# Sending the last seventeen weight blocks of a mixture-of-experts tail from the ScalarE queue

## What is computed

```python
hn2 = _layernorm(x, ln2_g, ln2_b).reshape(-1, h)
logits = hn2 @ gate_w + gate_b
idx = jnp.argmax(logits, axis=-1)
mid = jax.nn.relu(jnp.einsum('th,ehf->etf', hn2, w1) + b1[:, None, :])
y = jnp.einsum('etf,efh->eth', mid, w2) + b2[:, None, :]
moe = y[idx, jnp.arange(hn2.shape[0])]
return x + moe.reshape(b, s, h)
```

## Time and profile before

| | |
|---|---|
| median of 3 timed runs | 705.04 us (702.55 to 707.58) |
| profiled execution, its own time | 702.71 us |
| span in the profile | 701.0 us |
| mean granted TensorE clock | 0.927 |

### The profile page before, as it was taken

The page is one execution under the profiler, slowest core; times in us unless marked ns, Lnnn a source line. Parts: engine busy times, 40 slices in busy tenths (PEclk is TensorE's granted clock), DMA queues, the critical chain, the costliest instruction groups (busy, mean ns, idle before and its releaser), DMA issues.

```text
span 701.0 us, 16358 instructions
## 1 busy us (share of the span) xinstructions
PE 570.1 (81%) x5771; PEld 339.1 (48%) x5771; DVE 480.9 (69%) x1356; ACT 425.4 (61%) x650; POOL 416.7 (59%) x443
## 2 busy tenths in 40 slices
PE   2648888888888878888897898878997899888992
PEld 1324333344445444455454554545553555557992
DVE  3546757868678868587867768687777787635452
ACT  1675376676785666757677596756675654534661
POOL 2469573648486953775757585769544235525664
PEclk9969779899999988799999999899998999999996
DMA  6420000000000100000012301001002022186650
GB/s 146 135 69 2 8 1 9 2 24 1 9 2 25 40 2 6 5 16 10 17 41 62 85 9 36 1 20 60 25 29 62 12 69 91 39 257 183 187 149 6
DMA packets 30143, 34.30 MB, mean 49 GB/s; under 512 B 6970, under 2 KB 21984, under 8 KB 30064
## 3 DMA queue, kind: packets, MB, share of 16 engines
q1 hardware_dynamic: 26096, 25.53, 12.9%
q0 software_dynamic: 2816, 6.43, 2.6%
q10 hardware_dynamic: 1152, 1.30, 0.6%
HBM read 22.37 MB, written 11.27 MB: 48 GB/s over the span
## 4 chain that ended last, share of the span: by engine, by line
PE 40%; DVE 23%; POOL 16%; issue 10%; ACT 7%; SPq 2%; DMA 1%; POOLq 0%; ACTq 0%; DVEq 0%
DVE mx L1230 10%; PE out L877 6%; POOL rs L1411 5%; PE ring_s L863 3%; POOL stack L1414 3%; PE out L762 3%; PE ring_p L943 3%; PE ring_p L701 3%; PE ring_s L843 3%; POOL p L1430 2%; ACT p L1004 2%; PE ring_p L814 2%; ACT p L973 2%; PE ring_s L749 2%; PE ring_p L931 1%
## 5 line engine op out<-in xcount | busy, mean ns | idle before, releaser
L1230 DVE TENSOR_REDUCE mx<-ring_s 128x4 f32<-128x1024 f32 x128 | 152.8, 1218 | 26.9 <-PE ring_s L843 26.1
L1004 ACT ACTIVATE p<-ring_s 128x1024 f32<-128x1024 f32 x128 | 126.3, 1027 | 38.8 <-PE ring_s L863 38.3
L973 ACT ACTIVATE p<-ring_s 128x1024 f32<-128x1024 f32 x96 | 97.1, 1022 | 38.5 <-PE ring_s L749 38.1
L1411 POOL TENSOR_TENSOR rs<-ms,small 128x40 f32<-128x40 f32 x14 | 94.8, 6772 | 27.6 <-DVE ms L1093 27.3
L1414 POOL TENSOR_SCALAR stack<-stack 128x256 f16<-128x256 f16 (+1 forms) x96 | 65.0, 700 | 75.7 <-DVE stack L1222 42.8
L1430 POOL TENSOR_SCALAR_AFFINE_SELECT p<-p 128x512 f32<-128x512 f32 (+1 forms) x96 | 75.8, 798 | 56.4 <-ACT p L977 56.3
L977 ACT ACTIVATE p<-p 128x1024 f32<-128x1024 f32 x96 | 100.2, 1057 | 0.7
L701 PE MATMUL ring_p<-blank 128*128 128x256 f16 x362 | 80.6, 286 | 5.1 <-ACT t_midT L1037 1.9
L877 PE MATMUL out<-p,v 128*32 128x256 f32 x1024 | 69.8, 400 | 1.3 <-DVE rb L1288 1.2
L843 PE MATMUL ring_s<-kc,qs 32*128 32x256 f16 x512 | 51.2, 281 | 20.2 <-DVE mx L1230 13.0
L863 PE MATMUL ring_s<-qs,kc 32*128 32x256 f16 x512 | 49.4, 290 | 10.1 <-DMA qs<-mT 4.5
(11 more groups left out here) (162 smaller groups left out, 1111.5 us busy)
## 6 DMA issues: line engine op xcount, KB each, us to landing
w_up<-in_L_ffn_w SPq DMA_DIRECT2D x40, 256.0 KB, 2.8
t_row<-routed_rows SPq DMA_DIRECT2D x40, 132.0 KB, 2.4
routed_rows<-padrow SPq DMA_DIRECT2D x8, 396.0 KB, 3.2
xs<-in_L_attn_x SPq DMA_DIRECT2D x16, 128.0 KB, 2.2
routed_rows<-padrow SPq DMA_DIRECT2D x8, 132.0 KB, 1.9
qs<-mT SPq DMA_DIRECT2D x64, 2.0 KB
out<-t_y,t_idx POOLq DMA_INDIRECT x40, 2.4
b_down<-in_L_ffn_b SPq DMA_DIRECT2D x1, 512.0 KB, 4.8
```

The costliest lines, as they stand in the source:

```text
L973: nc.scalar.activation(p1[:, u], bank(f"b_sc{u}", n)[:], ACT.Tanh, scale=float(ISQ / CAP)).then_inc(b_s.sem, 1)
L1004: nc.scalar.activation(p2[:, u], bank(f"e_sc{u}", n)[:], ACT.Exp, scale=float(ISQ)).then_inc(e_s.sem, 1)
L1230: nc.vector.tensor_reduce(mx2[:, t, 2 * pair:2 * pair + 2, 2 * k:2 * k + 2], bank(f"d_mx{j}", n)[:].rearrange("p (z g s) -> p z g s", z=2, ...
L1411: nc.gpsimd.tensor_tensor(rs1[:], ms1[:], half, ALU.pow).then_inc(a_p.sem, 1)
```

## The change

The up weights of tiles 23 to 39 are no longer sent by SyncE (`g_w`) but by ScalarE, in a new step `g_wa`. It waits for the plan and for the up product of tile s-8, as `g_w` does, reads the expert's number into a ScalarE register, sends the transfer, and keeps the register; `g_mid` of the same tile then uses it and does not read the number again.

```diff
-ONLY = dict(a_root=tuple(range(ROOTS)), a_pow=tuple(range(ROOTS, B)), p_bT=(0,), p_bTc=(0,), p_plan=tuple(last for last, *_ in PLANS), q_sp=(PLANS[-2][0],))
+ONLY = dict(g_w=tuple(range(PLANS[-1][1])), g_wa=tuple(range(PLANS[-1][1], SLOTS)), a_root=tuple(range(ROOTS)), a_pow=tuple(range(ROOTS, B)), p_bT=(0,), p_bTc=(0,), p_plan=tuple(last for last, *_ in PLANS), q_sp=(PLANS[-2][0],))
...
+            expert = {}
+
+            def g_wa(s):
+                act.wait_ge(r_v.sem, r_v.upto(LAST, "row"))
+                wait(act, up_t, s - 8, "x")
+                expert[s] = act.value_load(slots[0:1, 0, s:s + 1], min_val=0, max_val=E - 1)
+                act.dma_start(w_up[:, s % 8, :], w1_d[bass.ds(expert[s] * P, P), :]).then_inc(w_in[s % 8], 16)
+
             def g_mid(s):
                 if s == 0:
                     act.wait_ge(bias_s.sem, bias_s.upto(0, "x"))
-                e = act.value_load(slots[0:1, 0, s:s + 1], min_val=0, max_val=E - 1)
+                if s in expert:
+                    e = expert[s]
+                else:
+                    e = act.value_load(slots[0:1, 0, s:s + 1], min_val=0, max_val=E - 1)
...
+    "g_wa": (2630, 2631, 2638, 2651, 2657, 2695, 2698, 2708, 2710, 2729, 2741, 2758, 2769, 2782, 2800, 2811, 2830),
```

More of the change, by code:

```diff
@@ new lines @@
+    "a_sum": (7, 24, 82, 131, 277, 421, 543, 708, 879, 1025, 1183, 1314, 1458, 1667, 1825, 1933),
+    "a_xT": (9, 14, 22, 102, 130, 286, 408, 569, 726, 937, 1051, 1179, 1309, 1503, 1658, 1807),
+    "a_qkv": (12, 19, 57, 124, 232, 382, 534, 687, 840, 1000, 1132, 1287, 1437, 1628, 1789, 1900),
+    "a_root": (15, 31),
+    "a_split": (16, 39, 98, 191, 297, 437, 595, 747, 909, 1112, 1215, 1393, 1536, 1697, 1860, 1992),
+    "a_qT": (23, 51, 118, 220, 319, 462, 614, 771, 943, 1122, 1246, 1416, 1594, 1734, 1876, 2017),
@@ new lines @@
+    "g_w": (1487, 1506, 1562, 1633, 1634, 1642, 1816, 1821, 2106, 2148, 2183, 2205, 2251, 2253, 2276, 2291, 2297,
+        2540, 2541, 2546, 2555, 2633, 2640),
+    "g_hTc": (1514, 1535, 1674, 1703, 1765, 1868, 1943, 1993, 2128, 2221, 2332, 2336, 2405, 2440, 2464, 2473, 2474,
+        2564, 2567, 2598, 2608, 2637, 2652, 2666, 2676, 2696, 2703, 2709, 2716, 2720, 2730, 2736, 2754, 2780, 2785,
+        2794, 2802, 2822, 2840, 2844),
+    "g_hT": (1519, 1533, 1673, 1688, 1770, 1852, 1923, 1979, 2120, 2231, 2338, 2342, 2401, 2442, 2458, 2467, 2471,
+        2568, 2582, 2601, 2614, 2628, 2648, 2663, 2678, 2688, 2707, 2714, 2723, 2735, 2740, 2748, 2760, 2772, 2776,
+        2784, 2796, 2805, 2817, 2826),
@@ new lines @@
+    "g_up": (1542, 1560, 1707, 1843, 1907, 1962, 1991, 2099, 2152, 2304, 2352, 2364, 2411, 2449, 2480, 2507, 2534,
+        2589, 2592, 2620, 2624, 2642, 2667, 2682, 2689, 2706, 2718, 2725, 2737, 2745, 2753, 2761, 2768, 2777, 2788,
+        2804, 2813, 2829, 2835, 2838),
+    "g_mid": (1546, 1547, 1709, 1857, 1908, 1957, 2001, 2097, 2165, 2298, 2345, 2379, 2423, 2447, 2478, 2518, 2533,
+        2573, 2581, 2617, 2626, 2650, 2670, 2683, 2700, 2702, 2715, 2724, 2734, 2749, 2750, 2765, 2781, 2793, 2798,
+        2812, 2842, 2845, 2851, 2853),
@@ new lines @@
+    "g_down": (1645, 1654, 1799, 1864, 1989, 2092, 2110, 2115, 2182, 2312, 2388, 2433, 2450, 2497, 2525, 2552, 2558,
+        2593, 2616, 2625, 2636, 2658, 2685, 2693, 2712, 2721, 2739, 2752, 2755, 2766, 2767, 2775, 2783, 2792, 2808,
+        2818, 2831, 2836, 2848, 2855),
+    "g_z": (1653, 1668, 1822, 1886, 2002, 2085, 2118, 2124, 2227, 2318, 2400, 2448, 2463, 2503, 2544, 2557, 2561,
+        2599, 2611, 2644, 2649, 2659, 2681, 2684, 2691, 2704, 2719, 2743, 2746, 2757, 2763, 2779, 2790, 2791, 2814,
+        2823, 2827, 2847, 2849, 2858),
@@ new lines @@
+    "g_rs": (1694, 1761, 1850, 1949, 2019, 2078, 2130, 2170, 2224, 2392, 2395, 2454, 2456, 2510, 2520, 2559, 2577,
+        2585, 2635, 2646, 2660, 2668, 2680, 2692, 2694, 2728, 2733, 2738, 2770, 2771, 2787, 2799, 2810, 2815, 2819,
+        2832, 2837, 2843, 2852, 2860),
+    "g_y": (1721, 1846, 1911, 1969, 2051, 2091, 2210, 2242, 2271, 2421, 2434, 2498, 2506, 2528, 2554, 2578, 2609,
+        2634, 2645, 2647, 2653, 2661, 2686, 2699, 2713, 2717, 2732, 2751, 2762, 2764, 2778, 2786, 2806, 2820, 2824,
+        2828, 2846, 2850, 2857, 2859),
@@ L308 @@
+    "g_out": (1797, 1906, 1946, 2027, 2084, 2129, 2261, 2373, 2413, 2476, 2488, 2509, 2512, 2516, 2574, 2580, 2606,
+        2664, 2665, 2675, 2687, 2690, 2701, 2711, 2722, 2731, 2747, 2756, 2774, 2797, 2803, 2809, 2816, 2821, 2834,
+        2839, 2841, 2854, 2856, 2861),
+    "q_sp": (2613,),
+    "g_wa": (2630, 2631, 2638, 2651, 2657, 2695, 2698, 2708, 2710, 2729, 2741, 2758, 2769, 2782, 2800, 2811, 2830),
 }
@@ L1042, in _ @@
             parts = dict(a_xTc=a_xTc, c_sum=c_sum, c_oTc=c_oTc, d_xTc=d_xTc, d_mTc=d_mTc, f_sum=f_sum, f_oTc=f_oTc,
-                         f_hTc=f_hTc, p_bTc=p_bTc, g_hTc=g_hTc, g_mid=g_mid)
+                         f_hTc=f_hTc, p_bTc=p_bTc, g_hTc=g_hTc, g_mid=g_mid, g_wa=g_wa)
             numbered(parts, "b_tanh", 6, b_tanh)
```

161 lines of the change are left out of this document (64 added, 97 removed), and 171 rows, old and new, of the table ORDER.

## The result

| | before | changed |
|---|---|---|
| median, four runs of each on one chip | 703.79 us (701.01 to 707.58) | 715.34 us (713.87 to 717.77) |
| profiled execution: own time, span | 702.71, 701.0 us | 713.87, 712.1 us |

The ratio is 1.0164, with a 95% interval from 1.0106 to 1.0222: slower by 11.6 us, and 3.3 us outside the range of the forecast. On another chip the same two kernels turned out level; that comes with the experiments.

A forecast was written before the change was run, and what follows sets the result against it. TensorE was taken as next to full in the tail, no single cost as the steady part's bound. Terms -0.3 + 1.4 + 0 + 0 - 2 = -0.9 from 702.7 gave 701.8; with 2.3 for timed runs, 704 us, range 696 to 712.

The forecast's parts named there:

- What bounds the kernel: Tail: TensorE next to full, 2.48 us a tile, no waits for weights; steady part: no one cost is the bound.
- SyncE's relief: Tail: SyncE loses 17 weight sends, worth nothing for weights; tile 23's row-block wait shrinks by 0 to 1.1 us, taken as -0.3.
- ScalarE's sends, +1.4 us: Tail: 17 sends on ScalarE at mean net 0.33 us each, a quarter of it reaching TensorE: +1.4 us.
- The rival that made them the tail's bound: Tail: each of the 17 sends delays g_hTc or g_mid by 0.65 us, +11 instead of +1.4: 714 us, chance 0.12.
- the fillers' rival: Ahead of batch 7's maxima: some 36 more fillers cost their 8 us, without the clock's gain: 714 us; 0.06 with unlucky order.
- The order at the last plan: VectorE: up 20's wait for g_z of tile 18 goes, the plan comes later; 1.8 us gained against 1.8 lost, 0.
- Pads: SyncE's q_sp comes 3.5 us later behind three more sends; spare before the last scatter shrinks from 4.1 to 0.6 us: 0.
- Fillers and clock from 40 to 100 us: Start: more and earlier fillers raise TensorE's low clock, 7.8 us less busy time, a quarter of it taken: -2 us.
- The rest of the order: 0: All engines: new order not priceable by rows; work ahead of each batch's maxima differs by at most 22 steps: 0, several us each way.
- the case that would put the result down to the steady part: Sign of being wrong: the last plan moves by more than 5 us, so the steady part's order, not any term, made the result.

The follow-up runs named there:

- queue_only: Kernel before, old order, with only the 17 weight sends of tiles 23 to 39 moved to ScalarE: 1.0000 of the kernel before, then 1.0016 on chip 9.
- plan_first: Changed kernel with VectorE's last plan put ahead of g_y of tile 16 and g_z of tile 18: 0.9940 of the kernel before, again (plan_first_2) 1.0161.
- the clean pair on chip 5: Changed kernel with VectorE's last plan ahead of g_y(16) and g_z(18), 713.5 us; the same with the old order up to the third plan, 426 fillers, 705.1 us.
- fill_gaps: Changed kernel with 26 more fillers where TensorE idles between the row maxima of batches 6 and 7: 0.9938 of the kernel before, on chip 15.
- after_filled: Changed kernel with 61 more fillers at 22 places where TensorE idled over 0.7 us between 150 and 610 us: 0.9946 of the kernel before, chip 4.

## Why the prediction was wrong

**What bounds the kernel, ScalarE's sends behind tile 23: right. SyncE's relief: right for the old order.** Tiles 23 to 39 take 39.7 us between their up products, as before. No wait for weights shows in the tail, one send step costs ScalarE 1.49 - 0.35 = 1.14 us, as the term said, and in the old order SyncE's queue is no limit: in `queue_only` the move alone is 1.000. The Trainium skill ("DMA: Bandwidth & Descriptors", section "Issuing engines are not separate DMA queues") said that sending from several engines saves only the sequencer's time. In the old order the runs agree (1.000 and 1.002). In the new order the move was worth 5 us (722.5 against 727.5), and not by the sequencer's time: two sends that wait for the last plan stood in SyncE's queue ahead of the weights of tile 21, which TensorE then lacked for 3.54 us.

**ScalarE's sends, +1.4 us: the term is not what was lost.** The rival that made them the tail's bound falls; its 714 us and those of the fillers' rival lie near the 715.3 by luck. The pair ahead of tile 21's `g_hTc` costs ScalarE 2.38 us of idle time and TensorE 0.19 us in the first trace, none in `plan_first_2`; the sixteen tiles behind pay nothing. In the old order, where other steps stand around them, up 20 to up 23 takes 11.8 and 10.7 us in the two `queue_only` traces against 8.1 to 9.6 without them, so 1 to 3 us, which the medians can't tell from nothing.

**The order at the last plan: wrong by what it counted.** I set 1.8 us gained against 1.8 lost on VectorE. The plan came 2.9 us later relative to the rank, and no gain showed: up 20 comes 4.9 us behind the rank, where it was 5.0. But the delay is hardly on the path (0.5 to 0.8 us by `plan_first_2`), so the net 0 stood for reasons that weren't mine. What I missed is TensorE's own order behind it: down 20 ahead of up 21 and down 21 ahead of up 22, about 3 us, and half clock behind them, about 2. The prediction compared no rows of TensorE's queue there.

**Pads: right.** 1.4 us to spare, near the 0.6 forecast.

**Fillers and clock from 40 to 100 us: the gain of 2 us didn't come.** The changed kernel's stretches, answering to the earlier trace rows:

```profile
40.00:60.00 20.00, 13.15 (x83) 6.68 (x76) 10.01 (x26) 12.12 (x15) 16.82 (x14) 0.66 0.18 61
60.00:80.00 20.00, 14.98 (x154) 7.80 (x153) 15.25 (x35) 10.75 (x14) 15.74 (x15) 0.83 0.03 9
80.00:100.00 20.00, 16.91 (x179) 9.18 (x182) 14.39 (x35) 11.58 (x16) 13.28 (x9) 1.00 0.03 8
100.00:120.00 20.00, 17.16 (x178) 7.58 (x170) 14.71 (x24) 12.57 (x16) 10.01 (x15) 0.84 0.01 2
```

One stretch rose from 0.76 to 1.00, the next fell from 0.92 to 0.84, and batch 3 is level in both (179.8 and 179.5 us). I had priced the clock where it was low and not asked where it would fall instead. The rival that priced the fillers at 8 us falls too: with 39 fewer nothing changes.

**"The rest of the order: 0": the step that failed.** Its price in the steady part is +6.9 us in the first pair of traces and 8.4 us in the medians of the clean pair on chip 5, and the tail's start adds 4.8. In the first pair the 6 us net arise between batches 6 and 7, half of them gone with fillers and a higher clock, half the steps. I had counted only the steps ahead of each batch's maxima, which can't see it: the count differs by at most 22 of 2415, and says nothing of who waits for whom. The text named this as the case that would put the result down to the steady part (last plan moved by more than 5 us; it moved by 9.7), but gave it no more than a share of 0.06 with the fillers, and my range stopped at 712.

**That one chip stands for all** was taken without a word. On four chips the kernel before is at 722 to 728 us, and the changed one was level where it was measured (once, on chip 9); in the two comparisons where it is at 703 to 704 (chip 5, and one that may be the same) the changed one loses 1.3 to 1.6%.

Still open: what the pauses are; which steps make the order's 3 us between batches 6 and 7, and the swing up to batch 11; why `d_nm` of batch 7 lasts 1.07 us; what `fill_gaps` is worth on a chip without pauses; and why the kernel before is at 728 us on chip 13. The loss of the sends taken out of the new order was never measured on a chip at 703 us. No kernel was shown to beat the old one where that runs at 703 us. `fill_gaps` and `after_filled` beat it by 0.5 to 0.6% on chips where it runs at 722 to 723, `plan_first` by 0.6% where it runs at 728.

## What to carry to other kernels

When a change brings a whole new order, "as much work ahead" doesn't price it: compare the order of the engine that bounds the stretch, step by step, and keep some 1% each way for the rest. Follow an idle time to the engine on the path before pricing it: 2.38 us of ScalarE were 0.19 us of TensorE. In an in-order queue look for a send that waits for something late and stands ahead of one that doesn't: it cost 3.5 us of TensorE here. And run the unedited pair again on another chip before explaining a percent; here both sides moved, one by 18 us and the other by 7.

## What was not expected of the hardware

The same program took 702.9 and 703.8 us in two comparisons and 722.2 to 728.0 on four other chips. Most of the difference begins at the same steps each time, where two or three engines stand still together for 1.5 to 2.7 us for nothing in the program. Time at half clock isn't lost time by itself: 24 us less of it brought 0 us in the old order, 4 us in the new (720.5 to 716.5 in span, on two chips).
